# Four-layer graph network with a recurrent layer: first twelve finished states turned to rows by the DMA queue as 16-bit planes, with reordered first groups and a last group in halves

## The reference

```
h = relu(layernorm(x)); x = x + attention(h, adj, W, a)        # 4 heads, leaky relu, masked softmax
h = relu(layernorm(x)); x = x + ((1+eps)*h + adj @ h) -> relu(. @ W1 + b1) @ W2 + b2
h = relu(layernorm(x)); x = x + adj @ (h @ weight) + bias
h = relu(layernorm(x))
for l in range(5):                                             # recurrent layer
    agg = (adj != 0)^T @ (h @ weight[l])
    r, z = sigmoid(gates of agg and h)
    n = tanh(i_n + r * h_n)
    h = (1 - z) * n + z * h
x = x + h * mask
```

## Time and profile before

| | us |
|---|---|
| runs | 636.84, 634.36, 635.74 |
| median | 635.74 |
| profiled execution | 636.28 |
| its span | 634.4 |
| PE busy | 607.7 (96%) |
| DVE busy | 525.4 (83%) |
| ACT busy | 553.2 (87%) |
| POOL busy | 402.3 (63%) |

### The profile page before, as it was taken

One profiled execution on the slowest core, in us unless ns is written; L12 is line 12 of the kernel. 1 busy time (PEld: TensorE's weight loads), 2 busy tenths in 40 slices (PEclk: granted clock), 3 DMA queues, 4 the chain that ended last, 5 costly groups with the idle time before them and its releaser, 6 DMA issues. The chain is left out here.

```text
span 634.4 us, 14614 instructions
## 1 busy us (share of the span) xinstructions
PE 607.7 (96%) x5070; PEld 387.2 (61%) x5070; DVE 525.4 (83%) x1312; ACT 553.2 (87%) x1042; POOL 402.3 (63%) x361
## 2 busy tenths in 40 slices
PE   5899999999999999999999999999999999999994
PEld 3567778788888887556545455555555555554552
DVE  6678898988888888889979888888788787787875
ACT  4688899999999999787988888898988889888883
POOL 3456777778877877367577656555565655555564
PEclk9999999999999999999999999999999999999998
DMA  8101011111100000224322324334243423335332
GB/s 182 49 4 54 18 48 32 52 40 33 52 20 18 19 19 1 51 51 62 57 50 51 67 51 85 71 78 80 56 83 67 84 56 80 67 68 84 70 81 67
DMA packets 113643, 35.79 MB, mean 56 GB/s; under 512 B 86625, under 2 KB 113570, under 8 KB 113570
## 3 DMA queue, kind: packets, MB, share of 16 engines
q1 hardware_dynamic: 113424, 34.79, 26.4%
q10 hardware_dynamic: 146, 0.07, 0.0%
HBM read 9.67 MB, written 4.19 MB: 22 GB/s over the span
## 5 line engine op out<-in xcount | busy, mean ns | idle before, releaser
L53 PE MATMUL psum<-h_parts,gru_w 128*128 128x512 f16 x720 | 182.5, 379 | 1.0 <-DVE r L1792 0.8
L53 PE MATMUL psum<-t_parts,gru_w 128*128 128x512 f16 x720 | 181.5, 379 | 0.0
L1751 POOL TENSOR_TENSOR h0T<-r,zh 128x512 f32<-128x512 f32 x80 | 101.6, 1270 | 107.2 <-DVE r L1788 107.1
L1745 POOL TENSOR_TENSOR zh<-z,h0T 128x512 f32<-128x512 f32 x80 | 103.9, 1299 | 34.2 <-ACT z L1720 33.8
L53 PEld LDWEIGHTS psum<-h_parts,gru_w 128*128 128x128 f16 x720 | 69.8, 98 | 82.7 <-DVE r L1792 4.2
L53 PEld LDWEIGHTS psum<-t_parts,gru_w 128*128 128x128 f16 x720 | 66.8, 98 | 66.5 <-DVE t_parts L1775 1.7
L1633 DVE TENSOR_TENSOR h_parts<-h0T,h_parts 128x512 f16<-128x512 f32 x80 | 65.1, 813 | 38.9 <-ACT h_parts L1620 38.7
L1717 ACT CAST t_parts<-psum 128x512 f16<-128x512 f32 x80 | 46.8, 585 | 35.8 <-PE psum L53 35.8
L720 POOL TENSOR_TENSOR prob<-prob,row_max 128x512 f32<-128x512 f32 x64 | 64.5, 1040 | 10.9 <-DVE row_max L1327 10.4
L1775 DVE TENSOR_TENSOR t_parts<-psum,t_parts 128x512 f16<-128x512 f32 x80 | 55.1, 689 | 18.9 <-ACT t_parts L1717 16.6
L1720 ACT ACTIVATE z<-psum,gates_b 128x512 f32<-128x512 f32 x80 | 62.2, 778 | 5.7 <-PE psum L53 0.9
(11 more groups left out here) (148 smaller groups left out, 1126.1 us busy)
## 6 DMA issues: line engine op xcount, KB each, us to landing
x_all<-in_x SPq DMA_DIRECT2D x16, 256.0 KB, 3.8
adj<-in_adj SPq DMA_DIRECT2D x16, 256.0 KB, 3.0
out_x<-y SPq DMA_DIRECT2D x14, 256.0 KB, 2.5
h_nodes<-h_parts SPq DMA_TRANSPOSE x80, 3.1
out_x<-zT SPq DMA_DIRECT2D x2, 256.0 KB, 2.3
gw<-in_L_gnn_weight SPq DMA_DIRECT2D x1, 320.0 KB, 5.4
W<-in_L_gnn_W SPq DMA_DIRECT2D x2, 128.0 KB, 3.1
wi<-in_L_gnn_w_ih SPq DMA_DIRECT2D x1, 192.0 KB, 5.5
```

The costliest lines, as they stand in the source:

```text
L53: return nc.tensor.matmul(out, lhsT, rhs, start=start, stop=stop)
L1745: pool.tensor_tensor(by_graph(zh[now.s][:, :]), by_graph(z[now.s][:, :]), state(now), ALU.mult)\
L1751: pool.tensor_tensor(state(now), by_graph(r[now.s][:, :]), by_graph(zh[now.s][:, :]), ALU.add)\
```

## The change

Four things change.

1. **The first twelve finished states.** PE's transposes, the PSUM bank and the one finish are gone for them. In place of these, ACT copies the state's 32-bit numbers as two planes of 16 bits (`take_half`, one plane at the end of each of two slots), SP issues a second transposing DMA (`turn_halves`), DVE puts the planes together again (`put_half`, one in each of two slots), and then does the four finishing operations in two pairs, in two further slots (`finish_turned`), from SBUF. The store is three slots later than the state.
2. **The last four states.** PE's transposes stand later in the slot (behind the z gate), and the finish one slot later. For the last one, POOL's add, the transposes, the finish and the store are made in halves, and the add is on DVE (`last_mix`, `last_back`, `last_finish`).
3. **The first groups.** In slots 2 to 7 work is put in another order: the scores of three graphs ahead of the mask of graph 3 in slot 3, the subtraction of graph 3's maximum on DVE for the first two groups (`less_last`), the turns of the weights and of adj and the fused products spread over slots 2 to 7, the row maxima over slots 5 to 10 and the scale in slots 11 to 13 (before 6 to 8).
4. **Every slot of the first part.** On DVE the copy of graph 3's `probT` stands ahead of the shift.

The core of the diff (items 2 and 3 cut to their main lines; of the new order only the lines that the text speaks of):

```diff
         def slot(at, number):                                  # DVE, first part
...
+            if at(3):
+                keep_probT(at(3), 3)
             if at(4):
                 shift_of(at(4), 1)
-            if at(3):
-                keep_probT(at(3), 3)
...
+        def less_last(group):                                  # DVE, groups 0 and 1
+            g = GROUP - 1
+            dve.wait_ge(max_done, group.graph_count(g))
+            v.tensor_tensor(prob[:, g, :, :], prob[:, g, :, :],
+                            top[:, g, :].unsqueeze(2).to_broadcast([128, HEADS, NODES]),
+                            ALU.subtract).then_inc(last_shifted, 1)
...
             if at(2) and number > 2:                           # PE, first part
                 mask(at(2), 2)
+            if number == 3:
+                scores(at(2), 0, GROUP - 1)
+            if at(2) and number > 2:
                 mask(at(2), 3)
...
+            if number == 3:
+                scores(at(2), GROUP - 1, GROUP)
...
             if number == 3:
                 project(at(2))
+                turn_y0(at(1))
+                gru.turn(pe, 2)
                 gru.fuse(pe, 0)
-                gru.fuse(pe, 1)
-                gru.fuse(pe, 2)
...
             if number == 5:                                    # DVE, first part
-                gru.row_max(dve, 4, 6)
+                gru.row_max(dve, 0, 1)
+            if number == 6:
+                gru.row_max(dve, 1, 2)
...
+    halves, halves_nodes, last_h = first.y[3], first.adjT1[0], first.adjT
...
+    def halves_of(x):
+        return x.bitcast(U16).rearrange("p g (n t) -> p t g n", t=2)
...
-            if ended is not None:                              # PE, recurrent
-                back(ended)
...
             remaining(j)
+            if j == SLOTS * ROUNDS + STREAMS - 1:
+                last_back()
+            elif j >= SLOTS * ROUNDS:
+                back(ended)
...
+        def take_half(group, half):                            # ACT, recurrent
+            act.wait_ge(h_ready, group.h_count)
+            if group.count > 1:
+                act.wait_ge(halves_landed, 16 * (group.count - 1))
+            a.copy(halves[:, 2 * half:2 * half + 2, :].bitcast(U16).rearrange("p u (v n) -> p (u v) n", v=2),
+                   halves_of(t["h0T"][:, bass.ds(group.first, GROUP), :])[:, half, :, :]).then_inc(halves_ready, 1)
...
+            for half in range(2):                              # ACT, end of slot
+                if ended_at(j + 3 - half):
+                    take_half(ended_at(j + 3 - half), half)
...
+        def put_half(group, half):                             # DVE, recurrent
+            dve.wait_ge(halves_landed, 16 * group.count)
+            v.tensor_copy(halves_of(last_h[group.count % 2][:, :, :])[:, half, :, :],
+                          halves_nodes[:, 2 * half:2 * half + 2, :].bitcast(U16)
+                          .rearrange("p u (v c) -> p (u v) c", v=2)).then_inc(last_h_ready, 1)
+
+        def finish_turned(group, half):
+            dve.wait_ge(last_h_ready, 2 * group.count)
+            dve.wait_ge(stored[0], group.to_store)
+            for g in range(2 * half, 2 * half + 2):
+                last = v.scalar_tensor_tensor(out[group.buffer][:, g, :], last_h[group.count % 2][:, g, :],
+                                              t["mask"][:, bass.ds(group.first + g, 1)],
+                                              t["x"][:, group.first + g, :], ALU.mult, ALU.add)
+            if half == 1:
+                last.then_inc(out_ready, 1)
...
+        def last_mix(two):
...
+            for k in range(2):
+                cols = slice(k * half * NODES, (k + 1) * half * NODES)
+                v.tensor_tensor(r[two.s][:, cols], r[two.s][:, cols], zc[two.s][:, cols], ALU.mult).then_inc(half_mixed, 1)
+                dve.wait_ge(half_mixed, k + 1)
+                v.tensor_tensor(t["h0T"][:, bass.ds(two.graph + k * half, half), :],
+                                r[two.s][:, cols].rearrange("p (g n) -> p g n", g=half),
+                                zh[two.s][:, cols].rearrange("p (g n) -> p g n", g=half), ALU.add).then_inc(half_ready, 1)
...
-            if ended_before(j, 1):                             # DVE, after the sum
+            for half in range(2):
+                if ended_at(j - half):
+                    put_half(ended_at(j - half), half)
+                if ended_at(j - 2 - half):
+                    finish_turned(ended_at(j - 2 - half), half)
+            if j > SLOTS * ROUNDS:
                 finish(ended_before(j, 1))
...
+        def turn_halves(group):                                # SP
+            sp.wait_ge(halves_ready, 2 * group.count)
+            if group.count > 1:
+                sp.wait_ge(last_h_ready, 2 * (group.count - 1))
+            sp.dma_start_transpose(halves_nodes[:, :, :].bitcast(U16).rearrange("p u (v c) -> p (u v) c", v=2),
+                                   halves[:, :, :].bitcast(U16).rearrange("p u n -> p (u n)")).then_inc(halves_landed, 16)
```

More of the change, by code:

```diff
@@ L39 @@
 FIRST_PARTS = 2
+TURNED = GROUPS - STREAMS
+U16 = mybir.dt.uint16
 LAST = GROUPS - 1
@@ L243, in keep @@
         elif lot == 2:
-            last = a.copy(self.gf[:, GRU_STEPS, :], bank[:, 0:384])
+            last = a.copy(self.gf[:, GRU_STEPS, :], P[:, B_EDGE, 0:384])
         else:
@@ L857, in mask, with scores @@
                gone[group.odd][:, g, :].unsqueeze(1).to_broadcast([128, HEADS, NODES]), True, False)
-        def scores(group):
+        def scores(group, first=0, end=GROUP):
             pe.wait_ge(e_lo, group.count)
-            for g in range(GROUP):
+            for g in range(first, end):
                 rows = slice(g * ROWS, (g + 1) * ROWS)
@@ L1135, in exponential @@
         def exponential(group, g):
-            act.wait_ge(shifted, group.graph_count(g))
+            if g == GROUP - 1 and group.number < SHARED:
+                act.wait_ge(last_shifted, group.count)
+            else:
+                act.wait_ge(shifted, group.graph_count(g) - min(group.number, SHARED))
             a.activation(prob[:, g, :, :], prob[:, g, :, :], ACT.Exp, scale=t["gates_b"][:, E_UNSCALE:E_UNSCALE + 1])\
@@ L1661, in back @@
             pe.wait_ge(h_ready, group.h_count)
-            if group.count > 1:
-                pe.wait_ge(out_ready, group.count - 1)
-            else:
-                pe.wait_ge(first.h0T_kept, GROUPS)
+            pe.wait_ge(out_ready, group.count - 1)
             for g in range(GROUP):
@@ L1670, in back, with last_back @@
             last.then_inc(back_psum, 1)
+        def last_back():
+            last, half = last_ended(), GROUP // 2
+            for k, bank in enumerate(HALF_BANKS):
+                pe.wait_ge(half_ready, k + 1)
+                if bank == BACK:
+                    pe.wait_ge(out_ready, last.count - 1)
+                for g in range(half):
+                    done = nc.tensor.transpose(P[:, bank, g * 128:(g + 1) * 128],
+                                               t["h0T"][:, last.first + k * half + g, :], t["ident"][:, :])
+                done.then_inc(half_back, 1)
         def slot(at, s, ended, j):
@@ L1746, in slot @@
                     .then_inc(zh_ready, 1)
+                if now.count == SLOTS * ROUNDS:
+                    return
                 pool.wait_ge(mixed, now.count)
@@ L1769, in finish, with last_finish @@
             last.then_inc(out_ready, 1)
+        def last_mix(two):
+            dve.wait_ge(cand_ready, two.count)
+            dve.wait_ge(zc_ready, two.count)
+            dve.wait_ge(zh_ready, two.count)
+            half = GROUP // 2
+            for k in range(2):
[5 more added lines that the diff above has]
+                                zh[two.s][:, cols].rearrange("p (g n) -> p g n", g=half), ALU.add).then_inc(half_ready, 1)
+        def last_finish():
+            last, half = last_ended(), GROUP // 2
+            for k, bank in enumerate(HALF_BANKS):
+                dve.wait_ge(half_back, k + 1)
+                for g in range(half):
+                    n = k * half + g
+                    done = v.scalar_tensor_tensor(out[last.buffer][:, n, :], P[:, bank, g * 128:(g + 1) * 128],
+                                                  t["mask"][:, bass.ds(last.first + n, 1)],
+                                                  t["x"][:, last.first + n, :], ALU.mult, ALU.add)
+                done.then_inc(half_out, 1)
         def slot(at, s, ended, j):
@@ L1784, in slot @@
                 state_parts(dve, now)
-            if two:
+            if two and two.count == SLOTS * ROUNDS:
+                last_mix(two)
+            elif two:
                 dve.wait_ge(cand_ready, two.count)
@@ L1793, in slot @@
                     .then_inc(gated, 1)
-            if ended is not None and ended.count > GROUPS - STREAMS:
-                finish(ended)
+            if j == SLOTS * ROUNDS + STREAMS - 1:
+                last_finish()
```

273 lines of the change are left out of this document (186 added, 87 removed).

## The result

The changed kernel takes 650.71 us (median of four runs, 650.24 to 651.22), against 636.13 for the kernel before beside it (a fourth run with the three of the table above): a ratio of 1.0236, with a 95% interval of 1.0221 to 1.025. I had forecast 637.2 and a range of 628 to 646. It is slower by 14.6, and the forecast is wrong. The profiled execution has a span of 649.4, 15.0 more than before.

A forecast was written before the change was run, and what follows sets the result against it. PE was taken to bound the kernel from about 360 us on, with ACT also full before. +8.7 − 2.5 − 3.8 − 0.9 = +1.5 on the profiled 636.28, with the median 0.54 lower, gave 637.2 us, range 628 to 646.

The forecast's parts named there:

- What bounds it: Whole run: PE busy 96%; PE bounds from about 360 us on, ACT and PE both full in the first 262.
- Part A: Slots 5 to 16: probT copy ahead lets POOL's add hold the shift, each slot 15.88 us: +8.7 us.
- Part B: First groups: reordered work takes three things off the path, and slot 4 has room for their return: −2.5 us.
- The three waits: Ahead of slot 4's activations: PE's wait for attended x 0.79, fused-weight products 0.81, their ACT copies 0.94; together 2.54 us.
- The cover for the weights' work: First part: moved row maxima and scale run on DVE and POOL beside PE and ACT, put at nothing.
- Part C: Twelve states turned by DMA: PE saves 5.3 us, held finishing operations from SBUF cost 1.5: −3.8 us.
- Rival 4: Extra transposing DMA delays the one PE waits for: 12 delays of about 0.6, +7, 644 us; chance 0.05.
- Rival 2: Recurrent part: the DVE and POOL loop becomes the bound, copies held by POOL's zh: 649 us; chance 0.10.
- Rivals 1 and 3: Shift not held, 625 to 629 us, chance 0.17; PE's turns leave but waits replace them, 641 us, chance 0.08.
- Part D: Tail, last mix to last finish, in halves: 1.7 us less at best, half taken: −0.9 us.

The follow-up runs named there:

- the exchange alone: The kernel before with only DVE's two instructions exchanged, the copy of graph 3's probT ahead of the shift: 643.18 us, 7.8 more than the kernel before.
- before_guarded: The kernel before with one edit, POOL's add of the self loops made to wait for the shift (the guard): 632.56 us.
- take_earlier: The changed kernel with both of ACT's 16-bit copies of a finished state made one slot earlier: 637.99 us.
- The wait alone: The changed kernel with SP still waiting for ACT's second copy but issuing no DMA for the state: 638.03 us.
- the issue alone: The changed kernel with ACT's copies a slot earlier and the state's DMA issued directly ahead of the next slot's transpose: 643.30 us.
- shift_guarded: The best kernel: the changed one with copies a slot earlier, shift ahead of the probT copy, and POOL's add waiting for the shift: 628.33 us.

## Why the prediction was wrong, point by point

- **What bounds it.** Right as far as it was traced: the two losses showed as waits of PE and of ACT, in different parts of the run.
- **Part A.** Right in place and near in size (+8.3 for +8.7; 7.8 for the exchange alone). The mechanism holds: the shift ends with POOL's add in 11 slots of 11, and is held by it in ten. That the size came so near has some luck in it: the steady slots take 15.65 and not 15.88, and slots with weight work up to 16.30 made up for it. And I gave the whole to the hold; with the hold gone, the later place in DVE's list alone still costs 3.5 of the 9.7.
- **Part B.** The three waits left the path, and more (−4.55 at slot 4), and 2.6 were given back in slot 4: −2.0 for −2.5. That the sum is near is luck: I had −2.5 leaving and nothing coming back. It is also a loose number, since the three kernels with the old order, alike up to there, take 13.7 to 16.2 for slot 2. The cover for the weights' work was wrong: with the guard in both, what the new order gains up to slot 5 it hands back by slot 17, and the best kernel owes its 4.2 over before_guarded to the recurrent part (381.3 against 386.0 from slot 17's leaky start to the last sum) and the tail.
- **Part C.** The step that failed is the sentence "The DMA is issued behind SP's own transpose of the slot and has two slots to land", which I put at no cost. SP's place was right, but not what it waits for there: I set down the ACT copies as 0.6 us on ACT and never asked when the second one ends, and who is queued behind the instruction that waits for it. It ends 0.4 to 1.1 after the next slot's `h_parts`, and behind it is the transpose that PE needs. Nor had the DMA two slots to land: at the first state DVE came to its `put_half` at 380.73, 1.8 after the issue and 1.4 before the landing. The wait alone costs nothing, the issue alone 5.3, both together 12.7 over take_earlier, since only what goes beyond the transpose's spare time, 1.05 to 1.6 by the estimate above, comes out as PE's wait. Without that step the term came out at −4.0 for −3.8, though its working had copies that are not held, and they are (below).
- **Rival 4** had the mechanism (the state's DMA delays the one PE waits for), and I gave it 0.05 and 644. Its argument against, one transpose a slot and slots of 4.33, counted SP's time and not its order. Its price, 0.6 a state, was too low: with the 12.7 us that it cost over take_earlier, 1.06 a state, my sum would have come to 637.2 + 12.7 = 649.9.
- **Rival 2** did not come: in take_earlier the recurrent part keeps its beat (the median from one `zh` on POOL to the next is 4.33), though its first assumption, that copies are held, was met (below); what POOL waited for z took it up. Rivals 1 and 3 did not come either.
- **Part D.** −0.3 for −0.9: the tail in halves has the third group's finish in between, and PE waits 1.5 for it ahead of its second half.

## What to carry to other kernels

A wait in an in-order DMA queue is priced by what stands behind it: for each added issue, set the time at which its producer ends beside the time at which the next entry becomes ready. Two losses in different parts can share a trace with gains of the same size, so undo each change by itself before judging the idea; here the DMA turning was good by 4.0 and one slot late. And where one engine holds another by issuing first, an order on the held engine's own list may not be enough: here a wait on the other one gave 4.2 more.

## What the runs showed of the hardware that was not expected

A copy with one operand is held too. `put_half` takes 0.46 when POOL stands still (above, at 382.24), and in take_earlier, beside POOL's `zh`, this:

```profile
380.76 1.27 POOL L1881 TENSOR_TENSOR zh<-z,h0T 128x512 f32<-128x512 f32 x1 [0.42 <-ACT z L1853]
380.98 1.37 DVE L1902 COPY adjT<-adjT 128x512 uint16<-128x512 uint16 x1
382.25 0.67 DVE L1747 TENSOR_TENSOR h_parts<-h0T,h_parts 128x512 f16<-128x512 f32 x1
```

Of 24 such copies the mean there is 1329 ns, and the finishing operations from SBUF, in pairs, take 742 each instead of 342 from PSUM. The Trainium skill says of it (SBUF — State Buffer, Who interferes with whom) that copies can enter a mode with two ports, when their operands meet its conditions, and then contend with GpSimd; the trace agrees, 1.37 against 0.46. The copy ends 0.32 after `zh`, not 0.68. All of it together cost at most 1.3 of the 5.3 us that PE saves in take_earlier (4.0 measured), and less in shift_guarded, where the same recurrent part is 4.9 shorter than before, from slot 17's leaky start to the last sum.
